# A two-layer mixture-of-experts kernel on one Trainium2 core: held weights in the shared experts, and routed results of layer 2 scattered to places by token

## The reference, cut to what matters

```
h = silu(x @ Wg[e].T) * (x @ Wu[e].T)          # width 176, for each chosen expert e
routed = sum over e of  c[token, e] * (h @ Wd[e].T)
shared = (silu(x @ Sg.T) * (x @ Su.T)) @ Sd.T  # width 352, for every token
f = routed + shared
```

## Time and profile before

| | |
|---|---|
| median of 3 runs | 1882.34 us |
| the profiled execution, its own time | 1864.71 us |
| its span | 1862.9 us |
| PE busy | 1756.0 us, 94% of the span |
| DVE, ACT, POOL busy | 1262.2 (68%), 908.8 (49%), 856.1 us (46%) |
| granted clock of PE, mean | 0.981 of full |
| chain that ended last | PE 77%, DVE 10%, POOL 5%, issue 3%, DMA 2%, ACT 2% |
| layer 0, shared tiles | about 463.5 to 563.8 us of the span |
| layer 1, routed blocks | 1567.9 to 1764.8 us |
| layer 1, shared tiles | 1764.8 to 1862.9 us |

### The profile page before, as it was taken

How to read it: one execution, slowest core, us unless ns; L and a number is a source line. 1 busy time by engine, 2 the same in 40 slices (tenths; PEclk the granted TensorE clock), 3 DMA queues, 4 the chain that set the end, 5 groups by cost and what they waited for, 6 DMA issues and landing times.

```text
span 1862.9 us, 34044 instructions
## 1 busy us (share of the span) xinstructions
PE 1756.0 (94%) x11310; PEld 1394.0 (75%) x11310; DVE 1262.2 (68%) x2787; ACT 908.8 (49%) x2986; POOL 856.1 (46%) x943
## 2 busy tenths in 40 slices
PE   5999998899888999999999999999999997999986
PEld 3666666677667888888888888888888885777754
DVE  4888888744567788887766767667666663444467
ACT  3767776544334444454454544544455442444422
POOL 2010014200566655666767677676776772000076
PEclk8999998999998999999999999999999998999999
DMA  7874643252420000000000000000001223333344
GB/s 237 267 260 143 211 133 114 69 153 92 161 78 25 1 12 1 1 7 7 15 21 15 21 15 15 21 18 24 15 12 46 80 80 132 106 107 108 97 139 124
DMA packets 104681, 148.21 MB, mean 80 GB/s; under 512 B 11888, under 2 KB 84720, under 8 KB 102096
## 3 DMA queue, kind: packets, MB, share of 16 engines
q1 hardware_dynamic: 95168, 119.95, 20.0%
q0 software_dynamic: 9216, 25.18, 4.1%
q10 hardware_dynamic: 144, 1.05, 0.2%
HBM read 81.64 MB, written 64.49 MB: 78 GB/s over the span
## 4 chain that ended last, share of the span: by engine, by line
PE 77%; DVE 10%; POOL 5%; issue 3%; DMA 2%; ACT 2%; SPq 0%; POOLq 0%; DVEq 0%; ACTq 0%
PE ps L1419 12%; PE ps L1434 9%; PE ps L1506 5%; PE ps L1952 5%; PE ps L1460 4%; PE ps L705 4%; PE ps L1448 3%; PE ps L1447 3%; PE ps L1446 3%; PE ps L959 3%; POOL work L2147 2%; PE ps L1441 2%; PE ps L1969 2%; PE ps L1971 2%; PE ps L724 2%
## 5 line engine op out<-in xcount | busy, mean ns | idle before, releaser
L1419 PE MATMUL ps<-work,weights 128*128 128x256 f32 x1024 | 248.4, 385 | 1.1 <-DVE work L1692 1.1
L1434 PE MATMUL ps<-split 128*128 128x512 f32 x768 | 227.5, 418 | 0.0
L1419 PEld LDWEIGHTS ps<-work,weights 128*128 128x128 f32 x1024 | 185.9, 191 | 22.3 <-DVE work L1692 1.3
L1834 POOL TENSOR_TENSOR work<-work,rope 128x512 f32<-128x512 f32 x128 | 164.4, 1285 | 53.0 <-ACT work L1607 53.0
L2147 POOL DMA_INDIRECT work<-yg,work x64 | 63.0, 984 | 226.9 <-DMA yg<-work 207.3
L1840 POOL TENSOR_TENSOR work<-work 128x512 f32<-128x512 f32 x128 | 164.4, 1284 | 5.0
L1434 PEld LDWEIGHTS ps<-split 128*128 128x128 f32 x768 | 130.8, 190 | 24.4
L827 DVE COPY work<-ps 128x384 f32<-128x384 f32 x256 | 130.0, 549 | 20.0 <-PE ps L705 19.7
L810 ACT ACTIVATE work<-ps,work 128x128 f32<-128x128 f32 x256 | 94.3, 368 | 86.2 <-DVE work L907 78.0
L705 PE MATMUL ps<-ident,work 128*128 128x128 f32 x768 | 116.6, 284 | 15.9 <-DVE work L827 14.0
L1506 PE MATMUL ps<-weights,work 128*128 128x256 f32 x512 | 124.0, 386 | 2.5 <-ACT work L1663 2.5
(11 more groups left out here) (240 smaller groups left out, 4411.7 us busy)
## 6 DMA issues: line engine op xcount, KB each, us to landing
heads_by_part<-split SPq DMA_DIRECT2D x64, 256.0 KB, 4.0
split<-heads_by_part SPq DMA_DIRECT2D x64, 256.0 KB, 3.2
work<-xg SPq DMA_DIRECT2D x118, 128.0 KB, 2.2
yg<-work SPq DMA_DIRECT2D x118, 128.0 KB, 1.7
xg<-work SPq DMA_DIRECT2D x13, 1024.0 KB, 5.8
weights<-in_w SPq DMA_DIRECT2D x8, 1024.0 KB, 7.1
weights<-in_f SPq DMA_DIRECT2D x8, 1024.0 KB, 5.1
weights<-in_f SPq DMA_DIRECT2D x8, 608.0 KB, 4.5
```

The costliest lines, as they stand in the source:

```text
L1419: last = pe.matmul(ps[:, 2, which * SEQ:(which + 1) * SEQ], w1(h, (which * KC + kc) * P, P), xT[:, kc, :], start=kc == 0, stop=kc == KC - 1)
L1434: last = pe.matmul(ps[:, 3, :], x1_split[:, xp, kc, c * P:(c + 1) * P], w_vg[:, n % 2, wp, kc, :], start=i == 0, stop=i == KC * len(TERMS) ...
L1834: pool.tensor_tensor(qk[:, h % 4, :, :], raw[:, h % 2, :, :], rope[:, 0, :].unsqueeze(1).broadcast_to([P, 2, SEQ]), ALU.mult).then_inc(rot ...
```

## The change

*Shared experts of both layers.* Gate and up now hold the weights in the array, in three chunks of 128, 128 and 96 columns, and stream the 128 tokens: the products come out with the hidden dimension on the partitions, so the three transposes and ACT's copy are gone. `shared_hidden` on DVE writes the down product's operand itself. Bank pairs 2, 3 and 4, 5 alternate by tile, and PE waits for the hidden values of two tiles back instead of one. The tanh and DVE's two operations cover 384 columns instead of 352.

*Layer 0, POOL.* `mix` stands ahead of `norm_pow` and `fetch`.

*Layer 1, routed results.* A table in DRAM, `ids1`, starts with a spare place per slot; POOL then scatters into it, for each (choice, tile), the place k * 2048 + token (`give_id`, 4 bytes a row): 32 of the 64 in the head pairs that have one row scatter, 32 behind attention. SP loads the table at block 22, PE turns it with the rows of block 26, ACT copies it and POOL makes integers. From there POOL scatters each block's result (`y4`, now a ring of 36) to its places in `yk1`, with three in flight, instead of SP's store. `fetch` becomes one plain DMA per tile, 4 x 128 rows, on POOL's queue. A constant `token_row` of 128 x 64 is loaded at the start. The layer 0 code changes in the shared expert as shown here for layer 1.

```diff
@@ -80,6 +80,7 @@
+RINGY1 = 12 * RINGY
...
@@ -1276,11 +1283,11 @@
                     norm1.pool_all(pool, 0)
+                if c >= 3:
+                    mix(c - 3)
                 if c >= 4:
...
                 fetch(c)
-                if c >= 3:
-                    mix(c - 3)
             norm_pow(TILES - 4)
...
@@ -1905,29 +1913,37 @@
-        y4 = carve("experts", RINGY, D)
-        h4 = carve("experts", 2, HCOLS)
+        h4 = carve("experts", 2, 2 * P)
...
-        th4 = carve("experts", 2, FS1)
+        th4 = carve("experts", 2, HCOLS)
...
+        y4 = carve("experts", RINGY1, D)
...
+        ids_rows = carve("experts", P, parts=NB1)
+        ids_f, ids_i = carve("experts", NB1), carve("experts", NB1, dt=mybir.dt.int32)
+        IDS_AT = 22
+        IDS_EARLY = 2 * (BATCH - 2) * PAIR1 - TILES * K1
...
@@ -1942,6 +1958,9 @@
                     last = pe.transpose(ps[:, n % 2, kc * P:(kc + 1) * P], x4[:, n % RINGX, kc * P:(kc + 1) * P], ident[:, :])
+                if n == IDS_AT + RINGX:
+                    pe.wait_ge(ids_loaded.sem, ids_loaded.at(0, 16))
+                    last = pe.transpose(ps[:, n % 2, D:D + NB1], ids_rows, ident[0:NB1, 0:NB1])
                 last.then_inc(x4_turned.sem, 1)
...
@@ -1972,21 +1991,28 @@
             def shared_gate_up(n):
+                bank = 2 + 2 * ((n - NB1) % 2)
                 pe.wait_ge(x4_copied.sem, x4_copied.at(0, n + 1))
-                pe.wait_ge(h4_ready.sem, h4_ready.at(0, n))
+                pe.wait_ge(h4_ready.sem, h4_ready.at(0, max(n - 1, NB1)))
+                if n == NB1 + 1:
+                    pe.wait_ge(h4T_copied.sem, h4T_copied.at(0, NB1))
                 for which in range(2):
-                    for kc in range(KC):
-                        at = (2 * kc + which) * FS1
-                        last = pe.matmul(ps[:, 2 + which, 0:FS1], xb4T[:, n % 2, kc * P:(kc + 1) * P], shared1[:, at:at + FS1],
-                                         start=kc == 0, stop=kc == KC - 1)
+                    for f in range(FS_CHUNKS):
+                        width = min(P, FS1 - f * P)
+                        for kc in range(KC):
+                            at = (2 * kc + which) * FS1 + f * P
+                            last = pe.matmul(ps[0:width, bank + which, f * P:(f + 1) * P], shared1[:, at:at + width],
+                                             xb4T[:, n % 2, kc * P:(kc + 1) * P], start=kc == 0, stop=kc == KC - 1)
                 last.then_inc(gu4_done.sem, 1)
...
             def shared_down(n):
-                pe.wait_ge(h4T_copied.sem, h4T_copied.at(0, n + 1))
+                pe.wait_ge(h4_ready.sem, h4_ready.at(0, n + 1))
                 pe.wait_ge(y4_copied.sem, y4_copied.at(0, n - 1))
...
                     at = 2 * KC * FS1 + f * D
-                    last = pe.matmul(ps[:, 6 + n % 2, 0:D], h4T[:, n % 2, f * P:(f + 1) * P], shared1[:, at:at + D],
+                    rows = min(P, FS1 - f * P)
+                    last = pe.matmul(ps[:, 6 + n % 2, 0:D], h4T[0:rows, n % 2, f * P:(f + 1) * P], shared1[0:rows, at:at + D],
                                      start=f == 0, stop=f == FS_CHUNKS - 1)
...
@@ -2018,7 +2044,6 @@
                     shared_down(n - 1)
-                turn_h(n, FS_CHUNKS)
             shared_down(UNITS1 - 1)
...
@@ -2026,25 +2051,22 @@
+                if n == IDS_AT + RINGX:
+                    act.copy(ids_f, ps[:, n % 2, D:D + NB1]).then_inc(ids_copied.sem, 1)
...
+                bank = 2 + n % 2 if n < NB1 else 2 + 2 * ((n - NB1) % 2)
...
-                act.activation(th4[:, n % 2, 0:width], ps[:, 2 + (n % 2 if n < NB1 else 0), 0:width], ACT.Tanh, scale=0.5)\
-                   .then_inc(th4_ready.sem, 1)
+                act.activation(th4[:, n % 2, 0:width], ps[:, bank, 0:width], ACT.Tanh, scale=0.5).then_inc(th4_ready.sem, 1)
...
-                if b >= RINGY:
-                    act.wait_ge(y4_stored[b % RINGY].sem, y4_stored[b % RINGY].at(0, 16 * (b // RINGY)))
-                act.copy(y4[:, b % RINGY, :], ps[:, 6 + b % 2, 0:D]).then_inc(y4_copied.sem, 1)
-            def copy_h(n):
-                act.wait_ge(h4_turned.sem, h4_turned.at(0, n + 1))
-                act.wait_ge(y4_done.sem, y4_done.at(0, n - 1))
-                act.copy(h4T[:, n % 2, :], ps[:, 4 + n % 2, 0:HCOLS]).then_inc(h4T_copied.sem, 1)
+                if b >= RINGY1:
+                    act.wait_ge(y4_spread[b % RINGY].sem, y4_spread[b % RINGY].at(0, 16 * ((b - RINGY1) // RINGY + 1)))
+                act.copy(y4[:, b % RINGY1, :], ps[:, 6 + b % 2, 0:D]).then_inc(y4_copied.sem, 1)
...
@@ -2061,31 +2083,35 @@
-                tanh(n, FS1)
+                tanh(n, HCOLS)
...
-                copy_h(n)
...
...
+            def shared_hidden(n):
+                bank, th = 2 + 2 * ((n - NB1) % 2), th4[:, n % 2, :]
+                dve.wait_ge(th4_ready.sem, th4_ready.at(0, n + 1))
+                dve.scalar_tensor_tensor(th, th, 1.0, ps[:, bank, 0:HCOLS], ALU.add, ALU.mult).then_inc(half4_step.sem, 1)
+                dve.wait_ge(half4_step.sem, half4_step.at(0, n + 1))
+                dve.wait_ge(y4_done.sem, y4_done.at(0, n - 1))
+                dve.tensor_tensor(h4T[:, n % 2, :], th, ps[:, bank + 1, 0:HCOLS], ALU.mult).then_inc(h4_ready.sem, 1)
...
@@ -2139,17 +2165,32 @@
+        def give_id(pool, n):
+            c, k = n // K1, n % K1
+            pool.indirect_dma_start(out=ids1[:, :], out_offset=bass.IndirectOffsetOnAxis(ap=route1.index[:, k, c:c + 1], axis=0),
+                                    in_=token_row[:, n:n + 1], in_offset=None).then_inc(route1.scattered.sem, 16)
         def pool_blocks1(pool):
...
                     pool.wait_ge(z4_ready.sem, z4_ready.at(0, c - 1))
-                for k in range(K1):
-                    pool.indirect_dma_start(out=yk4[:, c % 2, k, :], out_offset=None, in_=yg1[:, :],
-                                            in_offset=bass.IndirectOffsetOnAxis(ap=route1.index[:, k, c:c + 1], axis=0))\
-                        .then_inc(yk4_loaded[c % 2].sem, 16)
+                pool.dma_start(yk4[:, c % 2, :, :], yk1[0:K1 * TOK, :].rearrange("(k c p) d -> c p k d", k=K1, p=P)[c])\
+                    .then_inc(yk4_loaded[c % 2].sem, 16)
+            for n in range(IDS_EARLY, TILES * K1):
+                give_id(pool, n)
+            pool.wait_ge(ids_copied.sem, ids_copied.at(0, 1))
+            pool.tensor_copy(ids_i, ids_f).then_inc(ids_ready.sem, 1)
+            pool.wait_ge(ids_ready.sem, ids_ready.at(0, 1))
+            for b in range(NB1):
+                pool.wait_ge(y4_copied.sem, y4_copied.at(0, b + 1))
+                if b >= RINGY:
+                    pool.wait_ge(y4_spread[b % RINGY].sem, y4_spread[b % RINGY].at(0, 16 * (b // RINGY)))
+                pool.indirect_dma_start(out=yk1[:, :], out_offset=bass.IndirectOffsetOnAxis(ap=ids_i[:, b:b + 1], axis=0),
+                                        in_=y4[:, b % RINGY1, :], in_offset=None).then_inc(y4_spread[b % RINGY].sem, 16)
             for n in range(RINGY):
-                pool.wait_ge(y4_stored[n].sem, y4_stored[n].at(0, 16 * len(range(n, NB1, RINGY))))
+                pool.wait_ge(y4_spread[n].sem, y4_spread[n].at(0, 16 * len(range(n, NB1, RINGY))))
             for c in range(TILES):
...
@@ -2245,6 +2286,7 @@
                     load_pair(0)
+                    sp.dma_start(ids1.rearrange("(b p) o -> b (p o)", p=P), A["no_row"]).then_inc(ids_cleared.sem, 16)
...
@@ -2296,10 +2338,6 @@
-            def store_block(b):
-                sp.wait_ge(y4_copied.sem, y4_copied.at(0, b + 1))
-                sp.dma_start(yg1[b * P:(b + 1) * P, :], y4[:, b % RINGY, :]).then_inc(y4_stored[b % RINGY].sem, 16)
             sp.wait_ge(vg_done.sem, vg_done.at(SEQ_END, NH1))
...
@@ -2311,10 +2349,9 @@
                     load_block(b + RINGX)
-                if b >= 2:
-                    store_block(b - 2)
-            store_block(NB1 - 2)
-            store_block(NB1 - 1)
+                if b == IDS_AT:
+                    sp.wait_ge(route1.scattered.sem, route1.scattered.at(0, route1.at_all()))
+                    sp.dma_start(ids_rows, ids1.rearrange("(b p) o -> b (p o)", p=P)).then_inc(ids_loaded.sem, 16)
             x_out = out.rearrange("b (c p) d -> p (b c) d", p=P)
...
@@ -2362,9 +2399,13 @@
                     if t == SCATTER_FROM and pp == 1:
+                        pool.wait_ge(ids_cleared.sem, ids_cleared.at(0, 16))
                         pool.wait_ge(route1.slots_ready.sem, route1.slots_ready.at(0, 1))
                     at, pairs = (t - SCATTER_FROM) * PAIR1 + pp - 1, (BATCH - SCATTER_FROM) * PAIR1
-                    for n in range(at * TILES * K1 // pairs, (at + 1) * TILES * K1 // pairs):
+                    here = range(at * TILES * K1 // pairs, (at + 1) * TILES * K1 // pairs)
+                    if len(here) == 1:
+                        give_id(pool, 2 * at - here[0])
+                    for n in here:
                         c, k = n // K1, n % K1
...
```

(3 more changed lines are left out.)

87 lines of the change are left out of this document (47 added, 40 removed).

## The result

The kernel before took 1883.71 us (median; 1881.27 to 1889.08), the changed one 1923.55 (1921.67 to 1925.76). The ratio is 1.0213, 95% interval 1.0191 to 1.0235: 40 us slower, where 24 us faster was forecast.

A forecast was written before the change was run, and what follows sets the result against it. In the two shared-expert stages PE waits: on a POOL-DVE dependence ring in layer 0, on POOL's gathers in layer 1. Gains 9 + 15 = 24 us off the 1882.34 us median gave 1858.3 us, range 1850 to 1872.

The forecast's parts named there:

- Identifiers, late half: Layer 1 routed stage: 32 identifier scatters, 40 us on POOL, stay hidden; nothing queues late if they land within 15 us.
- rival 4: Layer 1 routed stage: slow-landing 4-byte rows hold SP at block 27 and PE stops; slower or nothing gained; chance 0.03.
- 79 stores leave SP's queue, 79 row scatters enter POOL's: Layer 1 routed stage: scatters at 1.3 us against 2.49 a block clear the backlog by about 1695, covered by PE.
- rival 3: Layer 1: scatters don't keep up because landing is slow, delaying the first loads; at 6.1 us landing 34 us slower; chance 0.05.
- the same 24 us: Whole kernel: the gain from the profiled execution, 1864.71 to 1840.7 us, also taken off the timed median of 1882.34.
- Identifiers, early half: Attention head pairs: 32 added identifier scatters cost nothing, with 0.37 us to spare in each 14.90 us step.
- Pace: Layer 1 last stage: DVE and PE tie at 4.23 us a tile, against 5.22; sign: either over 95% busy.
- The plain load: Layer 1 last stage: one load replaces four gathers, 4.0 us assumed, 2.5 to 6.2 possible; called the unknown price.
- rival 1: Layer 1: the plain load is dear and sets the pace; gain there 0 to 6.5, total 1870; chance 0.15.
- Start of the last stage: Layer 1: the first combine starts at 1778.3 against 1777.51 before, 0.8 us later.
- Layer 0: Shared-expert stage: mix leaves POOL's ring of dependences, PE becomes the bound at 4.84 us a tile; gain 9 us.
- Rivals 2 and 5: 2: layer 0 stays in its ring, 1864, chance 0.12; 5: held weights bring no lead, 1877, chance 0.02.

The follow-up runs named there:

- experiment 7: Kernel with held weights and earlier mix, plus 32 memsets: 0.9955; row scatters 2.6 us apart: 0.9969; four groups of eight: 0.9959; word scatters 2.6 us apart: 1.0219.
- experiment 9: The changed kernel as it stands, run again beside the kernel before on an F chip: 1891.80 us, ratio 1.0145.
- F chips: Label for the chips (or times) of the later runs, where the kernel before took 1861 to 1865 us.
- H chips: Label for the chips (or times) of the result and earlier experiments, where the kernel before took 1882.1 or 1884.8 us in the experiments.
- experiments 2 and 3: Changed kernel with fixed table replacing identifier scatters, results not sent to tokens; 2 reads it at block 22: 1879.84 us, 0.9994; 3 at block 0: 1850.84 us, 0.9842.
- experiments 1 to 5: 1: held weights and earlier mix only, 1880.94 us; 5: that plus 32 back-to-back transfers, words scattered 1928.21, rows scattered 1916.08, rows gathered 1919.39; 2 to 4: own lines.
- experiment 4: Changed kernel with the fixed table read at block 0, plus SP storing each output pair two tiles later: 1839.24 us, ratio 0.9774.
- experiments 7 and 8: 7: own line; 8: another F chip, held-weights kernel plus 32 back-to-back row scatters 0.9965, groups of eight 0.9968, paced rows 0.9968; kernel before 1861.3 us.

## Why the prediction was wrong

By its own steps. Two of them failed on the kind of chip that the result came from, and the first failed on both kinds:

- **"Identifiers, late half": hidden. This is the step that failed, with 41 us.** I counted POOL's time (40 us; it took 40.2) and SP's wait ahead of block 27, and asked only how long the words themselves might take. They slowed SP's transfers while they ran: 48 us for 32 of them in experiment 7, 41.7 us in experiment 9, both on F chips. SP loads one block of x per 2.49 us throughout this stage, and four loaded blocks were no cover for 44 us. The cover that I named, PE's 196 us, depends on those loads; PE was the victim, not the shelter. This was the ground of rival 4, to which I gave 0.03. I had put its place at blocks 26 and 27, where the table is read; the damage was done at the first blocks, and the table was read at 1654.9 without PE waiting for it.
- The Trainium skill's rule that I set beside that rival (DMA: Bandwidth & Descriptors, "Specifications": transfers under 512 B are read-modify-write) pointed the right way. The runs agree that such transfers are dear (48 us, experiment 7); that they are read-modify-write no run shows. What the rule doesn't say is where the cost fell, on the neighbours' packets, 0.63 us against 0.06.
- **"79 stores leave SP's queue, 79 row scatters enter POOL's": covered.** The second failed step. True on F chips (PE 30.00 of 30 us, experiment 9), false on H chips, where the backlog of scatters 1.27 us apart cost 29 us (experiments 2 and 3). (By my own 1.3 us a scatter the backlog lasts until 1702, not 1695; nothing hangs on it.) In rival 3 I had looked for a scatter that is slow itself. They kept up: POOL waited 6.4 us in all for a landing. Who was late was everybody else. No row of before could show it, for its profile, 1864.7 us beside timed runs of 1882, was that of an F chip by its time and by its last stage of 78.25 us. I took "the same 24 us" off the median and never asked what the 17.6 us between them were. That gap was the one sign in the data.
- **"Identifiers, early half": costs nothing.** From the first head pair to the last (start of the pair's power on POOL): 966.1 us before; after, 966.4 on the F chip, 972.8 on the result's, of which 2 to 4 us are also there without identifiers (968.0 to 970.6 in the H profiles of experiments 1 to 5). Right on F, 2 to 5 us short on H.
- **"Pace": 4.23 us a tile.** The result shows 71.7 us from first to last combine, 4.78 a tile, for a reason that I had not priced: SP's order (experiment 4). With that mended, 60.5 us, against 61.2 forecast, and 4.13 in the steady steps, with DVE over 95% busy (57.6 of 60.5 us), as the prediction's sign said. That step, once SP is out of the way, is right in its mechanism. I had costed SP's queue for what the change moves, and not for what a faster stage would ask of it: at the old 5.22 us a tile the token loads behind the output stores came in time, at 4.2 they don't.
- **The plain load**, my unknown price and rival 1: POOL spends 0.75 us on it, and DVE waits for one once, 4.2 us. Rival 1 falls. Landing within about 4 us fits; the trace has no landing time for it.
- **"Start of the last stage": 0.8 us later.** From the first transpose of the routed stage to the first combine: before 210.8 us (1566.7 to 1777.5), in experiments 3 and 4 211.0 (1556.4 to 1767.4) and 210.7. Right, within a microsecond.
- **Layer 0: 9 us.** Gate/up comes every 4.80 us (501.44 to 506.24; 4.84 forecast), and in the later part of the stage PE is never idle (37.0 of 37.0 us from 500 on, before 36.4 of 41.5 from 505 on): 5.1 us. But in the first 40 us PE still idles 4.4 us, as before; I had left 2 for the first gathers. DVE's waits on gathers there grew from 5.9 to 13.4 us. The combines gained 79.9 - 73.7 = 6.2 us in this profile. The seventeen profiles of kernels with this code give 70.6 to 74.1 us, half of them 71.7 or less, where the three of before have 79.9: a gain of 5.8 to 9.3, 8.2 in the middle. The mechanism was right, and the 9 about a microsecond too large. Rivals 2 and 5 fall with it: DVE's waits on the mix are gone from the list, and PE runs full.
- **Held weights in layer 1** brought nothing by themselves: on F chips the kernels of experiments 7 and 8 have a last stage of 78.1 to 78.9 us, the old 78.25, and their total of 0.9955 to 0.9969 (words left out), 6 to 8 us, is no more than layer 0's gain. The gathers set that pace, as the prediction said.

So the sum in parts, on H chips by ratios of about 1883 us: without identifiers, backlog and SP's order -42.6; SP's order +12.8; backlog +28.6; identifiers +41.2; together +40. The first of these is more than the 24 us forecast. What fits is that the kernel before itself loses some 20 us to the hold-up on H chips (its gathers leave in a run through the last stage, and four kernels with the same gathers took 98 to 103 us there for 78 on F chips), which paced scatters and plain loads don't. That is argued, not shown: before has no profile on an H chip. On F chips the changed kernel was 26.5 us slower (1891.80 against 1865.25) where 24 faster was forecast, a miss of 50 us, and the identifiers' 42 to 48 us are nearly all of it. The forecast for the profiled execution, 1840.7 us, was the time of experiment 4 (1839.2), but that is luck in part: it ran on an H chip, on which its gain by ratio was 43 us and not 24.

## What to carry to other kernels

Price a transfer by what it does to the others in flight, above all to the loads that a busy engine lives on; "hidden beside PE" holds only while PE's own loads arrive. Do not scatter 4-byte words beside loads that an engine waits for (some 40 to 48 us for 32 of them here): let an identifier ride with a row that moves anyway. Spread indirect transfers on GpSimd at the pace of the work where you can, and when a profile is 1% faster than the timed runs, find out why before you build on it.

## What was not expected of the hardware

- 32 indirect scatters of 128 words of 4 bytes cost 48 us, 1.5 us each, even 2.6 us apart. A load of 128 KB beside them took 17.4 us to land (35.7 with the scatters 1.26 us apart) in the place of 2.2.
- In the H runs, after some five to ten indirect transfers (scatters or gathers of 1 KB rows) issued 1.27 us apart, ACT, DVE and PE start their next instruction 8 to 20 us late (ACT 8.0 us again and again), though the DMA share is 0.31; 32 of them cost 35 us. In the F runs the same kernel loses nothing. Memsets on GpSimd do no harm on an F chip, and were not tried on the other kind. What is held up, and whether the chip or the moment decides it, stays open.
